# Experts of a mixture layer run before the last two rows of attention instead of behind all eight, and their results are gathered by token

## The chip, the core and the metric

The kernel runs on one core of a Trainium2 chip. The core has TensorE (PE, matrix products into PSUM), VectorE (DVE), ScalarE (ACT), GpSimd (POOL) and SyncE (SP, which here only issues transfers); they run their own instruction streams and meet through semaphores. The metric is the device time of one execution in microseconds (us), lower is better. The times below are medians of several executions; the trace comes from one profiled execution.

## What is computed

With x of 8 batch rows ("rows" below) of 512 tokens and 256 features, a layer norm feeds two branches that are both added to x: causal attention with 16 heads and a linear position bias, and a mixture of 8 experts.

```python
xn = _layernorm(x, axis=-1)
x = x + attn(xn, W_kqv, b_kqv, W_proj, b_proj, slopes) + ffn(xn, Wg, W1, W2)

# ffn, T = 4096 tokens, E = 8 experts, cap = T // E = 512
probs = softmax(xt @ Wg)
# every expert selects its cap likeliest tokens; a token goes to the likeliest expert
# that selected it, or to its likeliest expert if none did
out = sum over e of  where(tok2exp == e, weight, 0) * (gelu(xt @ W1[e]) @ W2[e])
```

Each token goes through exactly one expert, so the kernel sorts tokens by expert and computes 39 tiles of 128 sorted tokens (4096 tokens, up to 7 tiles of padding).

## The kernel before

**Start.** Layer norm of all rows, projections to keys, queries, values and the router's logits, each value split into a high and a low fp16 part. It ends 120.5 us into the trace, where the first exponential of attention starts.

**Eight rows of attention.** Each row has 4 groups of 4 heads, each group 10 slots (`NSJ`), so 40 slots a row. In a slot PE computes scores (`scores`, L1368), ACT takes their exponential into `pr_all` (L865), and in rows 0 to 5 POOL zeroes the part above the diagonal (L711, 7 selects a group); in rows 6 and 7 PE adds the mask to the scores itself (L1363). Slots of a later group hold the product with the values (`with_v`, L1388), transposes, the projection (L1418) and the residual add on DVE (L1052). In the same slots PE and DVE find the row maxima of the *next* row (`max_unit`, L1287 and L1293; `row_max`, L992 and L997), so row 7 has none of that work. Which slot holds what is a table; each engine's stream is in the order of the slots, and an engine that waits in one slot holds back all that is behind it in its stream.

**Work for the experts within the rows.** 32 quarters of expert weights are read, scaled by ACT (L834), split by POOL (`expert_high` L678, `expert_low` L682) and stored: 4 before row 0, then one a group in rows 0 to 6. DVE finds each expert's 512th chance by 15 bisection steps (`bisect_count`, `bisect_take`: 6 in row 0, 3 each in rows 1, 2 and 3), and then makes the routing, 18 pieces of small operations in rows 4 and 5 (`ROUTED = 4`). The list of sorted tokens is filled with empty entries by 10 DMAs of POOL in the start; then 32 scatters of POOL (indirect DMAs, 128 tokens each, L695) write normalized tokens with their number and weight into `sorted_rows`: four in a run behind each of the groups in `SCATTERS`, from (row 5, group 2) to (7, 1).

**Experts, behind row 7.** Per tile: SP loads a transposed tile (L488) and its 128 token numbers (L491), PE computes `up` (16 products, L1540 and L1541) and `down` (12 products, L1550), both with weight addresses from registers, and between them ACT and DVE pass five operations: `cross` (L889), `sum_up` (L1214), `gelu` (L895), `high` (L901), `low` (L1219). POOL gathers the 128 rows of x plus attention that belong to the tile (L744), DVE multiplies the result by the weight and adds them (`combine`, L1225), and POOL scatters the tile to the output (L750). `up` runs three tiles ahead of `down`. Hidden values use two pairs of PSUM banks; attention's buffers in `pr_all` hold the experts' inputs and results.

Of the kernel before, what the change touches and what calls it, by code (L numbers as in the profile page):

```python
# [22 lines left out]
AHEAD = 4  # L23
OUT_BANKS = (4, 6, 5, 7)
# [5 lines left out]
ROWS_FIRST = 3  # L30
ROWS_EARLY = 4
# [3 lines left out]
HG = 4  # L35
# [26 lines left out]
ROW = 2 * E + 4  # L62
BITS = 30
ROUTED = 4
SCATTERS = [(5, 2), (5, 3), (6, 0), (6, 1), (6, 2), (6, 3), (7, 0), (7, 1)]
PER_EXPERT = NT // X
FILLS = 10
FILLS_FIRST = 5

HALVES = 3  # L70
NO_TOKEN = 1 << 20
# [19 lines left out]
STEPS = [(0, u) for u in (1, 8, 15, 22, 29, 36)] + [(n, u) for n in range(1, ROUTED) for u in (2, 8, 14)]  # L91
# [15 lines left out]
GROUPS = NG * B  # L107
AWAY = GROUPS - 5


def values_at():
    pieces, copies, turns, scales, pairs, packs = ({} for _ in range(6))
    for y in range(GROUPS - 1):
# [6 lines left out]
        pieces[own_ + first], pieces[own_ + second] = (y, (0,)), (y, (1, 2, 3))  # L120
        copies[own_ + copy], turns[own_ + turn], scales[own_ + turn] = y, y, y
# [6 lines left out]
NQ = 4  # L128


def layer(nc, x, w_kqv, b_kqv, w_proj, b_proj, slopes, wg, w1, w2, out):
# [6 lines left out]
    out_rows = out.rearrange("b s e -> (b s) e")  # L138
    xa_t = xa_d.rearrange("(b t p) e -> b p t e", p=P, t=TB)

    with ExitStack() as ctx:
# [29 lines left out]
        x_last = tables[:, 0:TB * E].rearrange("p (t e) -> p t e", t=TB)  # L171
# [63 lines left out]
        def cut(n_bytes, dt, pattern=None, **dims):  # L235
# [15 lines left out]
        token = sb("token", [P, 8, 2], I32)  # L251
# [51 lines left out]
        pos_made, scattered, list_init, w1_in, w2_in = sem("pos_made"), sems("scattered", X), sem("list_init"), sem("w1_in"), sem("w2_in")  # L303
        xs_in, xT_in, h_made, hg_made, hh_made, hl_made, o_made, ob_made = (
            sems("xs_in", SLOTS), sems("xT_in", SLOTS), sem("h_made"), sem("hg_made"), sem("hh_made"),
            sem("hl_made"), sem("o_made"), sem("ob_made"))
        cross_out, h_summed = sem("cross_out"), sem("h_summed")
        xg_in, ob_out = sems("xg_in", SLOTS), sems("ob_out", SLOTS)
        consts = sem("consts")
        apart = sem("apart")  # L310
        zrows_in, bias_made, xb_made = sem("zrows_in"), sem("bias_made"), sem("xb_made")
        xr_made = sem("xr_made")
        x_last_in = sem("x_last_in")
# [8 lines left out]

        def wait_apart(eng, signal, value):
            eng.wait_ge(signal, value)
            eng.sem_inc(apart, 1)
# [25 lines left out]


# [11 lines left out]
        def _(sp):  # L364
# [96 lines left out]
            for n in range(B):  # L461
                for g in range(NG):
                    q = NQ * (n + 1) + g
                    if NQ < q <= NQ * X:
                        store_quarter(q - 1)
                    if NQ * X > q + 1 and q > NQ:
                        load_quarter(q + 1)
                    if g == 3 and n < B - 1:
                        shift_rows(n + 1)
# [25 lines left out]
            for q in range(ROWS_EARLY):  # L495
                load_rows(q, q)
                if q == 1:
                    store_sum(B - 2)
# [1111 lines left out]
```

## Time and profile before

| what | us |
|---|---|
| median of 3 executions (595.95 to 599.14) | 597.97 |
| span of the profiled execution, first to last instruction | 607.7 |
| start, to the first exponential of row 0 | 120.5 |
| rows 0 to 5 | 243.4 |
| rows 6 and 7 | 81.8 |
| last exponential of row 7 to the end | 162.0 |

The profiled execution's time is known by its span alone, which is 9.7 us over the median of the timed ones. Busy time in the span: PE 504.2, DVE 404.6, ACT 337.4, POOL 326.0. Boundaries of rows are the starts of their first exponential. In the trace, a number in square brackets is how long the engine had been idle before an instruction, and the arrow names what ended that; "remote" means that no instruction of the program ends at that moment, "issue" that the engine waited for nothing that the profile shows.

### The profile page before, as it was taken

Reading aid. Unit: us, or ns where it says so; the run is one execution under the profiler, and the core shown is the slowest. Engines: PE = TensorE matmul, PEld = TensorE weight load, DVE = VectorE, ACT = ScalarE, POOL = GpSimd, SP = SyncE. Lnnn points to the kernel's source line nnn. Section 1 sums busy time; section 2 is a strip of 40 time slices with the busy share of each in tenths; the row PEclk is TensorE's granted clock in tenths of the full one; section 3 lists DMA queues with packets and bytes.
Section 4 is the critical chain, followed back from the end, with each engine's and each line's share of the span. In section 5 each row is a group of like instructions: output and inputs, shape, how many; then the busy total and the mean of one; then the engine's idle time right before and its main releaser. Section 6 shows DMA issues by size and latency. Waiting matters only on the chain.

```text
span 607.7 us, 13176 instructions
## 1 busy us (share of the span) xinstructions
PE 504.2 (83%) x4807; PEld 288.6 (47%) x4807; DVE 404.6 (67%) x829; ACT 337.4 (56%) x640; POOL 326.0 (54%) x524
## 2 busy tenths in 40 slices
PE   1989996688889889899888898977897887887785
PEld 1555652233334444343434344433465676575664
DVE  5987769997998897987898976620124444354344
ACT  4455652165766676766757666555644444354343
POOL 4787634245535463644745568654413665555555
PEclk9999997558989999998999898998898898798889
DMA  8899998232413433525225238438355343333410
GB/s 264 266 243 269 303 310 267 91 92 62 126 62 115 148 118 100 149 79 146 84 84 148 81 105 254 151 101 310 114 106 124 100 107 83 94 94 100 94 56 35
DMA packets 94903, 85.59 MB, mean 141 GB/s; under 512 B 36883, under 2 KB 84883, under 8 KB 94831
## 3 DMA queue, kind: packets, MB, share of 16 engines
q1 hardware_dynamic: 82088, 59.64, 34.0%
q0 software_dynamic: 7360, 18.80, 10.4%
q10 hardware_dynamic: 5392, 6.31, 3.4%
q8 instruction: 39, 0.64, 0.4%
q14 instruction: 24, 0.20, 0.1%
HBM read 42.26 MB, written 37.95 MB: 132 GB/s over the span
## 4 chain that ended last, share of the span: by engine, by line
PE 50%; DVE 29%; issue 7%; ACT 6%; another core or an unknown queue 5%; POOL 3%; DMA 1%; ACTq 0%; DVEq 0%; POOLq 0%
DVE mx L997 12%; PE ps L1388 9%; PE ps L1256 8%; PE ps L1368 6%; PE ps L1550 6%; PE ps L1418 5%; PE ps L1540 4%; DVE mx L992 3%; PE ps L1541 3%; ACT pr_all L865 3%; PE ps L1293 3%; PE ps L1287 2%; PE ps L1398 2%; PE ps L1363 2%
## 5 line engine op out<-in xcount | busy, mean ns | idle before, releaser
L865 ACT ACTIVATE pr_all<-ps 128x512 f32<-128x512 f32 x320 | 179.1, 598 | 86.3 <-PE ps L1368 80.9
L997 DVE TENSOR_REDUCE mx<-ps 128x2 f32<-128x768 f32 (+1 forms) x192 | 156.9, 863 | 18.4 <-PE ps L1293 9.2
L711 POOL TENSOR_SCALAR_AFFINE_SELECT pr_all<-pr_all 128x256 f32<-128x256 f32 (+1 forms) x168 | 71.1, 451 | 115.2 <-ACT pr_all L865 115.1
L1368 PE MATMUL ps<-qs,ks 64*128 64x384 f16 (+3 forms) x512 | 108.6, 316 | 11.8 <-ACT pr_all L865 11.1
L1388 PE MATMUL ps<-pr_all,vt 128*17 128x512 f32 (+3 forms) x1024 | 88.3, 463 | 1.9 <-ACT pr_all L865 1.3
L1550 PE MATMUL ps<-vt,pr_all 128*128 x312 | 65.2, 295 | 20.3 <-DVE pr_all L1219 15.2
L1214 DVE TENSOR_TENSOR pr_all<-ps,pr_all 128x512 f32<-128x512 f32 x39 | 27.0, 691 | 75.2 <-ACT pr_all L889 52.9
L1293 PE MATMUL ps<-ks,qs 64*128 64x128 f16 (+3 forms) x512 | 76.8, 330 | 0.0
L1287 PE MATMUL ps<-step,pick 64*128 64x128 bf16 (+1 forms) x640 | 55.1, 223 | 22.9 <-DVE mx L997 15.6
L750 POOL DMA_INDIRECT out_dram<-pr_all,token x39 | 43.8, 1124 | 48.0 <-DVE pr_all L1225 32.7
L1540 PE MATMUL ps<-pr_all,xnp 128*128 128x256 f16 x312 | 61.6, 288 | 3.7 <-DVE pr_all L1214 2.7
L1541 PE MATMUL ps<-pr_all,xnp 128*128 128x128 f16 x312 | 58.4, 229 | 4.6 <-issue 4.6
L889 ACT ACTIVATE pr_all<-ps 128x512 f32<-128x512 f32 x39 | 23.1, 593 | 68.0 <-PE ps L1541 34.7
L1368 PEld LDWEIGHTS ps<-qs,ks 64*128 64x128 f16 x512 | 36.5, 98 | 51.0 <-ACT pr_all L865 38.0
L1287 PEld LDWEIGHTS ps<-step,pick 64*128 64x128 bf16 x640 | 27.5, 98 | 66.9 <-DVE mx L997 31.3
L744 POOL DMA_INDIRECT pr_all<-x_plus_attention,token x39 | 40.7, 1045 | 22.7 <-issue 11.6
L992 DVE TENSOR_REDUCE mx<-ps 128x4 f32<-128x1024 f32 x32 | 39.1, 1223 | 14.3 <-PE ps L1293 13.6
L1550 PEld LDWEIGHTS ps<-vt,pr_all 128*128 128x128 f16 x312 | 32.5, 105 | 29.3 <-DVE pr_all L1219 18.2
L1550 PE MATMUL ps<-w_low,pr_all 128*128 x156 | 45.8, 294 | 0.7 <-issue 0.7
L1388 PEld LDWEIGHTS ps<-pr_all,vt 128*17 128x17 f32 x1024 | 24.6, 99 | 37.4 <-issue 27.2
L1256 PE MATMUL ps<-pr_all,w_h 128*128 128x512 f16 x128 | 39.5, 391 | 1.3 <-ACT pr_all L783 1.3
L1540 PEld LDWEIGHTS ps<-pr_all,xnp 128*128 x312 | 32.3, 103 | 11.8 <-issue 6.5
(195 smaller groups left out, 885.2 us busy)
## 6 DMA issues: line engine op xcount, KB each, us to landing
qs<-q_parts SPq DMA_DIRECT2D x64, 100.0 KB
ks<-k_parts SPq DMA_DIRECT2D x64, 96.0 KB
sorted_rows<-ecmp POOLq DMA_DIRECT2D x10, 516.0 KB, 7.0
k_parts<-pr_all SPq DMA_DIRECT2D x16, 256.0 KB, 2.9
q_parts<-pr_all SPq DMA_DIRECT2D x16, 256.0 KB, 3.1
w_h<-in_L_ffn_W_dram SPq DMA_DIRECT2D x16, 256.0 KB
w_l<-in_L_ffn_W_dram SPq DMA_DIRECT2D x16, 256.0 KB
expert_parts<-w_low SPq DMA_DIRECT2D x32, 128.0 KB
```

The costliest lines, as they stand in the source:

```text
L711: pool.affine_select(out=v, in_=v, compare_op=ALU.is_ge, fill=0.0, base=0, pattern=[[0, blocks], [1, P]], channel_multiplier=-1).then_inc( ...
L865: act.activation(dst, src, ACT.Exp, scale=SCORE).then_inc(exp_made, 1)
L992: last = dve.tensor_reduce(mx[:, n1 % 2, :, 2 * g:2 * g + 2, 1], ps[:, 2 * (u % 2):2 * (u % 2) + 2, :].rearrange("p e (c n) -> p e c n", c=2),
L997: last = dve.tensor_reduce(mx[:, n1 % 2, :, 2 * g + c, t], ps[:, 2 * (u % 2):2 * (u % 2) + 2, c0:c0 + w], AX, ALU.max)
L1256: last = pe.matmul(out, lhs(a_, k), rhs(b_, k), start=(k == 0 and j == 0), stop=(k == EC - 1 and j == 2))
L1287: pe.matmul(dst[:, :, c0:c0 + HALF], pick64[own_half(e), h, :], step64[own_half(e), None, :].broadcast_to([HALF, len(ends), HALF]), start= ...
L1293: last = pe.matmul(bank[2 * (u % 2) + e][:, c0:c0 + w], qs[own_half(e), p1, 2 * g + i, P * t:P * (t + 1)], ks[own_half(e), p1, 2 * g + i, ...
L1368: last = pe.matmul(dst[:, c0:c0 + w], ks[rows, p, 2 * g + i, t * P:(t + 1) * P], qs[rows, p, 2 * g + i, t * P:S], start=not masked, stop=T ...
L1388: last = pe.matmul(bank[6][32 * h:32 * h + VW, t * P:S], vt[:, n, t, g * HG + h, :], pr_all[:, HG * (g % 2) + h, W_AT[t]:W_AT[t] + S - t * ...
L1540: pe.matmul(both, hi, xT[:, q8, k::EC, :], start=(k == 0), stop=(k == EC - 1), skip_group_check=True)
L1541: last = pe.matmul(own_, lo, xT[:, q8, k, :], start=False, stop=(k == EC - 1), skip_group_check=True)
L1550: last = pe.matmul(out[:, 0:E], hh[:, q, a_, f * P:(f + 1) * P], weights(w2_b[b_], e * W2_STEP + w2_at(f), E), start=(f == 0 and j == 0), ...
```

## The change

- The expert stage is moved between row 5 and row 6 (`SPLIT = 6`). It needs its routing sooner: the steps of the bisection are 6, 5, 4 in rows 0, 1, 2; all routing is in row 3 (`ROUTED = 3`); up to 6 quarters of weights a row in rows 0 to 3 and 4 in row 4.
- The 10 fills of the list follow the first 10 groups. The 32 scatters stand singly between the selects, four a group, in the groups (3, 3) to (5, 2). Token numbers and weights are no longer stored with the rows (`ROW` is 512 and not 516).
- In the expert stage POOL has no instruction. DVE copies each tile's result (`take_result`), and SP stores it to `sorted_results`, in sorted order.
- POOL waits until all 39 tiles are stored (`tiles_out`), then gathers 32 times 128 results by token, one every second slot of rows 6 and 7 (`GATHERS_AT`); six slots after its gather DVE multiplies by the weight and adds to x plus attention (`add_moe`, `MOE_AT`), reloaded to `sums` for rows 0 to 4. SP stores whole rows of the output.
- Before row 6 PE waits for the last results, ACT for `o_made`, and from the second group of row 6 ACT waits for `tiles_out`, since `pr_all` is shared.

```diff
+SPLIT = 6
-SCATTERS = [(5, 2), (5, 3), (6, 0), (6, 1), (6, 2), (6, 3), (7, 0), (7, 1)]
+SCATTERS = [(3, 3), (4, 0), (4, 1), (4, 2), (4, 3), (5, 0), (5, 1), (5, 2)]
+SCATTER_AFTER = (2, 5, 8, 10)
-STEPS = [(0, u) for u in (1, 8, 15, 22, 29, 36)] + [(n, u) for n in range(1, ROUTED) for u in (2, 8, 14)]
+STEPS = [(0, u) for u in (1, 8, 15, 22, 29, 36)] + [(1, u) for u in (2, 8, 14, 20, 27)] + [(2, u) for u in (2, 8, 14, 20)]
+GATHERS_AT = {at_slot(SPLIT, 2 * t): t for t in range(NT)}
+MOE_AT = {at_slot(SPLIT, 2 * t + 6): t for t in range(NT)}
...
# POOL, per group of rows 0 to 5
+                    def scatter_at(place):
+                        if (n, g) in SCATTERS:
...
+                            pool.wait_ge(exp_made, NSJ * G + SCATTER_AFTER[place])
+                            scatter(PER_EXPERT * SCATTERS.index((n, g)) + place)
...
# POOL, rows 6 and 7
+            def gather(t):
...
+                pool.indirect_dma_start(out=moe[t // (NT // 2)][:, t % (NT // 2), :], out_offset=None, in_=ys_d,
+                                        in_offset=bass.IndirectOffsetOnAxis(ap=pos[:, t:t + 1].bitcast(U32), axis=0)
+                                        ).then_inc(moe_in[t % SLOTS], 16)
+            add_bias(SPLIT - 1)
+            pool.wait_ge(tiles_out, 1)
...
# ACT
+                    if G == G_SPLIT:
+                        act.wait_ge(o_made, WORK)
+                    if G == G_SPLIT + 1:
+                        act.wait_ge(tiles_out, 1)
...
# DVE
+            def take_result(s):
...
+                dve.tensor_copy(ob[:, q, :], bank[OUT_BANKS[s % len(OUT_BANKS)]][:, 0:E]).then_inc(ob_made, 1)
...
# PE
+                if v in (NSJ * G_SPLIT, NSJ * G_SPLIT + 1):
+                    pe.wait_ge(ob_made, WORK - 2 + v % 2)
...
+            def experts():
+                turn_y(G_SPLIT - 2)
...
+                up(0, e[0])
+                with_v(G_SPLIT - 1, range(TB))
...
+                up(1, e[1])
+                turn_y(G_SPLIT - 1)
...
+                up(2, e[2])
+                turn_pair(G_SPLIT // 2 - 1)
```

Where work moves, in the order of the instructions. First POOL in row 4, one group with its selects (AFFINE_SELECT), its weight quarter (CAST, then TENSOR_TENSOR); `pos` is the list of places. Before:

```order
L711 AFFINE_SELECT pr_all<-pr_all 128x2x128 x3
L678 CAST vt<-w_h 128x512
L711 AFFINE_SELECT pr_all<-pr_all 128x2x128 x3
L711 AFFINE_SELECT pr_all<-pr_all 128x4x128
L682 TENSOR_TENSOR w_low<-w_h,vt 128x512
```

POOL in row 4, group 2, now:

```order
L716 DMA sorted_rows<-xnp,pos 5120x256
L730 AFFINE_SELECT pr_all<-pr_all 128x2x128 x3
L716 DMA sorted_rows<-xnp,pos 5120x256
L699 CAST vt<-w_h 128x512
L730 AFFINE_SELECT pr_all<-pr_all 128x2x128 x3
L716 DMA sorted_rows<-xnp,pos 5120x256
L730 AFFINE_SELECT pr_all<-pr_all 128x4x128
L716 DMA sorted_rows<-xnp,pos 5120x256
```

The same selects now have a scatter ahead of or behind each of them. Second, DVE at the routing's pieces `pick` to `choose` (operations on `rr`, `r` and `hit`), between the row maxima (`mx`). Before, in row 4:

```order
L1091 TENSOR_TENSOR rr<-rr,gtb 128x256
L997 TENSOR_REDUCE mx<-ps 128x2 x4
L1121 TENSOR_REDUCE r<-rr 128x32
L1091 TENSOR_TENSOR rr<-rr,r 128x256
L992 TENSOR_REDUCE mx<-ps 128x2x2
L997 TENSOR_REDUCE mx<-ps 128x2
L1042 RECIPROCAL rec<-ps 128x16
L1046 TENSOR_TENSOR yqp<-ps,rec 128x4x64
L1091 TENSOR_TENSOR rr<-rr,pr 128x256
```

The same pieces now, in row 3:

```order
L1110 TENSOR_TENSOR rr<-rr,gtb 128x256
L1140 TENSOR_REDUCE r<-rr 128x32
L1110 TENSOR_TENSOR rr<-rr,r 128x256
L1013 TENSOR_REDUCE mx<-ps 128x2
L1110 TENSOR_TENSOR rr<-rr,pr 128x256
L1145 SCALAR_TENSOR_TENSOR rr<-rr 128x256
L1149 TENSOR_REDUCE r<-rr 128x32
L1110 TENSOR_TENSOR rr<-rr,r 128x256
```

One row maximum stands where there were six. Third, PE where the expert stage now hands over to row 6, the last products of `down` and the first scores, masks and row maxima:

```order
L1542 MATMUL ps<-w_low,pr_all 128x256
L1542 MATMUL ps<-vt,pr_all 128x256
L1404 MATMUL ps<-id,late 128x64 x2
L1409 MATMUL ps<-qs,ks 128x512
L1326 MATMUL ps<-step,pick 128x64 x4
L1332 MATMUL ps<-ks,qs 128x512 x2
```

No product with the values stands in the first group of row 6, since that of row 5's last group is done within the expert stage.

## Rows read from the trace of the kernel before

**Rows 1.** Windows by stage: length, busy us by engine (instructions), granted clock, DMA share, GB/s.
```profile
core 0: us, PE busy (x) PEld busy (x) DVE busy (x) ACT busy (x) POOL busy (x), PEclk, DMA share, GB/s
...
161.70:203.40 41.70, 36.79 (x387) 17.22 (x387) 36.45 (x82) 27.09 (x51) 18.30 (x36) 0.96 0.33 102
203.40:242.70 39.30, 35.20 (x380) 16.61 (x380) 34.25 (x76) 27.20 (x52) 20.99 (x40) 1.00 0.41 124
242.70:281.90 39.20, 35.47 (x381) 16.66 (x381) 34.15 (x76) 27.09 (x52) 21.00 (x40) 1.00 0.38 113
281.90:324.10 42.20, 36.47 (x382) 16.70 (x380) 37.00 (x63) 27.09 (x51) 22.56 (x40) 0.96 0.35 102
324.10:363.90 39.80, 35.66 (x381) 16.98 (x381) 35.62 (x64) 27.22 (x52) 25.63 (x44) 0.96 0.37 110
363.90:408.50 44.60, 38.14 (x415) 19.27 (x415) 23.10 (x36) 27.07 (x51) 29.64 (x33) 0.96 0.53 175
408.50:445.70 37.20, 31.30 (x313) 14.39 (x313) 5.02 (x14) 24.02 (x47) 14.88 (x18) 0.91 0.57 190
...
460.60:602.60 142.00, 115.42 (x1046) 95.35 (x1044) 64.08 (x114) 65.04 (x113) 81.86 (x76) 0.91 0.35 88
```
**Rows 2.** Timeline of PE: first product of down for two tiles in a row.
```profile
543.67 0.27 PE L1550 MATMUL ps<-vt,pr_all 128*128 x1
...
546.30 0.27 PE L1550 MATMUL ps<-vt,pr_all 128*128 x1
```
**Rows 3.** Timeline of POOL, ACT and PE at one stop of the expert stage.
```profile
559.77 1.03 POOL L744 DMA_INDIRECT pr_all<-x_plus_attention,token  x1 [0.30 <-issue]
...
565.09 1.03 POOL L744 DMA_INDIRECT pr_all<-x_plus_attention,token  x1 [0.30 <-issue]
...
567.18 0.60 ACT L889 ACTIVATE pr_all<-ps 128x512 f32<-128x512 f32 x1 [4.87 <-remote]
...
562.69 0.22 PE L1541 MATMUL ps<-pr_all,xnp 128*128 128x128 f16 x1
```
**Rows 4.** Timeline of POOL and DVE in row 6: last of four scatters, next row maximum.
```profile
369.83 0.97 POOL L695 DMA_INDIRECT sorted_rows<-xnp,pos  x1 [0.30 <-issue]
...
371.80 1.29 DVE L997 TENSOR_REDUCE mx<-ps 128x2 f32<-128x768 f32 x2 [3.33 <-remote]
```
**Rows 5.** The chain that ended last, shares by line: expert stage, then rows 6 and 7.
```profile
by line: PE ps L1550 24.8%; another core or an unknown queue 17.3%; PE ps L1540 15.2%; issue 12.7%; PE ps L1541 11.4%; DVE pr_all L1214 5.9%; DVE pr_all L1219 5.3%; ACT pr_all L889 4.3%; ACT pr_all L901 1.7%; DVE pr_all L1225 1.1%; POOL out
...
by line: PE ps L1368 17.3%; PE ps L1388 15.3%; PE ps L1363 12.4%; ACT pr_all L865 10.1%; issue 9.9%; PE ps L1418 7.1%; another core or an unknown queue 6.9%; PE ps L1398 6.2%; PE ps L1293 5.3%; ACT ysb L839 3.8%; PE ps L1287 2.8%; PE ps L14
...
by line: PE ps L1388 19.2%; PE ps L1368 16.3%; issue 15.8%; ACT pr_all L865 14.5%; PE ps L1363 11.4%; PE ps L1418 10.4%; PE ps L1398 7.2%; another core or an unknown queue 4.9%; ACT ysb L839 2.3%; PE ps L1405 1.6%; ACT yqp L845 1.2%
```
**Rows 6.** Groups of DVE instructions in row 2: three bisection steps.
```profile
L1074 DVE TENSOR_SCALAR_CACHE_REDUCE hit<-rr,cand 128x256 bf16<-128x256 f32 x3 | 1.4, 479 | 0.1
...
L1084 DVE TENSOR_TENSOR thr<-thr,found 128x1 uint32<-128x1 uint32 x3 | 1.0, 335 | 0.1
...
L1070 DVE TENSOR_TENSOR cand<-thr,bits 128x3 uint32<-128x3 uint32 x3 | 0.6, 215 | 0.1
```
**Rows 7.** Groups of POOL instructions: row 4, and the scatters of rows 6 and 7.
```profile
L711 POOL TENSOR_SCALAR_AFFINE_SELECT pr_all<-pr_all 128x256 f32<-128x256 f32 (+1 forms) x28 | 12.8, 484 | 19.7 <-ACT pr_all L865 19.6
L691 POOL TENSOR_TENSOR xr<-xr,xb 128x256 f32<-128x256 f32 x4 | 2.8, 729 | 0.0
...
L682 POOL TENSOR_TENSOR w_low<-w_h,vt 128x512 f16<-128x512 f32 x2 | 2.3, 1156 | 0.0
...
L678 POOL CAST vt<-w_h 128x512 f16<-128x512 f32 x2 | 1.2, 606 | 0.0
...
L695 POOL DMA_INDIRECT sorted_rows<-xnp,pos x28 | 27.4, 978 | 10.2 <-issue 7.0 <-ACT pr_all L865 3.1
```
**Rows 8.** The end of row 7 in the chain and on DVE, and 256 KB stores' landing.
```profile
446.35 2.35 PE ps L1388 x32
448.70 1.92 PE ps L1418 x8
...
455.20 1.53 DVE L1236 TENSOR_TENSOR tables<-ps,tables 128x512 f32<-128x512 f32 x2 [1.91 <-PE ps L1418]
...
q_parts<-pr_all SPq DMA_DIRECT2D x16, 256.0 KB, 3.1
```

More of the change, by code:

```diff
@@ L698, in _ @@
             pool.wait_ge(bias_made, 1)
-            for part in range(FILLS_FIRST, FILLS):
-                empty_list(part)
             for q in range(NQ):
@@ L703, in _ @@
                 expert_low(q)
-            for n in range(B):
+            for n in range(SPLIT):
                 for g in range(NG):
@@ L773, in _ @@
+            add_bias(SPLIT - 1)
+            pool.wait_ge(tiles_out, 1)
+            for n in range(SPLIT, B):
+                for g in range(NG):
+                    for k in range(NSJ):
+                        if (n, g, k) in GATHERS_AT:
+                            pool.wait_ge(exp_made, NSJ * (NG * n + g) + k)
+                            gather(GATHERS_AT[n, g, k])
+                    if n == SPLIT and g > 1:
+                        add_bias(SPLIT + g - 2)
         @block.scalar
@@ L915, in _ @@
+            copy_y(NG * B - 1)
+            copy_pair(GROUPS // 2 - 1, slice(0, S // 2))
         @block.vector
@@ new lines, in experts, with add_moe @@
+            def experts():
+                scale(G_SPLIT - 2)
+                for s in range(HID):
+                    sum_up(s)
+                    low(s)
+                    if s == 0:
+                        scale(G_SPLIT - 1)
+                for s in range(WORK):
+                    if s + HID < WORK:
+                        sum_up(s + HID)
+                    if HID <= s + HID - 1 < WORK:
+                        low(s + HID - 1)
+                    take_result(s)
+            def add_moe(t):
+                n = t // TB
+                dve.wait_ge(moe_in[t % SLOTS], 16 * (t // SLOTS + 1))
+                if n < SPLIT - 1:
+                    dve.wait_ge(sums_in[n], 16)
+                elif n == SPLIT - 1:
+                    dve.wait_ge(xadd_made, t + 1)
+                else:
+                    dve.wait_ge(xr_made, n + 1)
+                rows = sum_rows(n)[:, t % TB, :]
+                dve.scalar_tensor_tensor(out=rows, in0=moe[t // (NT // 2)][:, t % (NT // 2), :], scalar=r32[:, 3, t:t + 1],
+                                         in1=rows, op0=ALU.mult, op1=ALU.add).then_inc(moe_added, 1)
@@ L1560, in _ @@
             pe.wait_ge(xadd_made, TB * (B - 1))
-            e = [expert(code[s // SLOTS], s % SLOTS) for s in range(WORK)]
-            find_up(0)
             with_v(NG * B - 1, range(TB))
```

549 lines of the change are left out of this document (271 added, 278 removed).

## The prediction, made before the changed kernel ran

> **What bounds the kernel now.** I read the busy time by stage first [rows 1]. In rows 2 and 3 of attention PE is busy 35.2 to 35.5 us and DVE 34.2 of some 39.2, and the length of a row follows DVE: 34.2 busy gives 39.2, 37.0 gives 42.2. Row 7, without row maxima, leaves DVE at 5.0 of 37.2. The expert stage, from the first `down` at 460.6 to the last at 602.6, takes 142.0 us for 39 tiles, 3.64 a tile. Two neighbouring tiles in the timeline start 2.63 apart, with PE full [rows 2]; 39 of those are 102.6. So 39 us of this stage are stops.
>
> The stops have one look [rows 3]. The last product of an `up` is recorded to end at 562.9, and ACT, which needs nothing more, starts only at 567.18, "remote", after 4.87 idle. POOL had issued five indirect DMAs without a pause, the last from 565.09 to 566.12: the stop ends 1.1 us after it. Row 6 has the same: four scatters, the last ending at 370.80, and a row maximum that begins at 371.80 after 3.33 idle [rows 4]. I found this end, 1.0 to 1.2 us behind a run of indirect DMAs, at every long stop I looked at in rows 6, 7 and the experts. In the chain these places are "unknown queue" and "issue", 17.3% and 12.7% of the expert stage, 6.9% and 4.9% "unknown queue" in rows 6 and 7 [rows 5]. My reading: PE's signals are held while POOL's indirect DMAs run in a row. What holds them I can't see.
>
> **The experts without POOL.** Between row 5's last exponential and row 6's first, PE has one `with_v` (2.35, [rows 8]), three sets of four transposes (some 0.6 each, an estimate from the fp32 products beside them), and 39 tiles by 2.63: 2.4 + 1.8 + 102.6 = 106.8. To that comes the first load of transposed rows, which SP issues only after `with_v` of group 22 (about 1.5), and at the end, where no `up` is left to cover them, the five operations from `up` to `down` (about 2), a copy and the first score (1): **112**. ACT and DVE have some 1.9 us a tile and stay below 2.63. SP's 128 KB store a tile is cheap to issue and nothing waits for it but `tiles_out`. The bounds are 108 (all ends overlap) and 151 (the 39 us stay).
>
> **The end.** From the last exponential at 445.7 to the last residual add at 456.7 [rows 8] are 11.0, of which `up` of two tiles took 3.0 of PE; they leave. Then a 256 KB store: 0.4 to issue and 3.1 to land [rows 8]. Tail: 11.0 − 3.0 + 3.5 = **11.5**. Before, the tail was inside the 162.0 behind row 7.
>
> **Rows 1 to 5, DVE.** One step of the bisection is three marks of 0.48, 0.34, 0.21 and two small ones: 2.3 us [rows 6]. Row 1 gets two more, +4.7; row 2 one more, +2.3. Row 3 loses three steps (−7.0), which leaves a bare 27.2; the routing, read as what rows 4 and 5 have over the bare load, is 9.8 + 8.4 = 18.2 [rows 1]. DVE in row 3 is then 45.4, 11.3 over now, and the row about 50.5. Rows 4 and 5 lose the routing, but they can't fall below PE's 35.5 and its gaps: I take 38.5 each, −3.7 and −1.3. Moving DVE's work costs because it's heaped: sum **+13.3**. If the heap in row 3 partly fills DVE's idle 5 us, it is +7.
>
> **Row 4, POOL.** Selects 12.8, bias 2.8, four quarters of 1.76, and 16 of the scatters at 0.98 plus the 0.30 of idle between them: 12.8 + 2.8 + 7.0 + 20.5 = 43.1 us [rows 7] in a row of 38.5. Each select stands behind a scatter, and `with_v` waits for the selects; POOL becomes the bound there: **+5**. Row 3 (4 scatters) and row 5 (12, no quarters: 31) stay under. The signals held by 32 single scatters: no row shows single ones. The bounds are 0 and the expert stage's 39 us over 78 indirect DMAs, 0.5 each, 16; I take **+2**, since in row 5 now four cost nothing visible against row 3 [rows 1]. ACT's and POOL's fills and quarters are covered: ACT is idle 12 us a row.
>
> **Rows 6 and 7** were 81.8. Out go one `with_v` (2.4, counted above) and the held signals behind runs of scatters, 6.9% of 44.6 and 4.9% of 37.2, 4.9 together. In come: (a) the restart. POOL's first gather waits for `tiles_out`, about 4 us after the last result, and lands some 3 later; DVE's first `add_moe` is six slots into row 6, about 5 us, and behind it stand row maxima that PE needs: +3. (b) 32 gathers of 1.03, one every second slot, that is, every 2 us: denser than single scatters, thinner than the runs. Bounds 0 and 0.5 each, 16: I take +5. (c) 32 adds of 0.48 on DVE, 15 us, hidden in its 21.5 and 32 idle us. Together 81.8 − 7.3 + 8 = **82.5**.
>
> **The sum,** against the trace's span: up to row 1 161.7; rows 1 to 5 202.2 + 13.3 + 5 + 2 = 222.5; experts 112; rows 6 and 7 82.5; tail 11.5. That is 590.2, 17.5 under 607.7. The timed executions have a median 9.7 below the span; I carry the difference over whole: 598.0 − 17.5 = 580.5, rounded to **581**. The start is left as it is: its last 23 us are DVE's row maxima, and the five fills taken from it are DMA work beside PE's.
>
> **Rivals.** *The stops stay* (ends slower). PE's stops would be a matter of its own stream in the expert stage, with addresses from registers, and not of POOL. Then the stage takes 151 rather than 112 and the time is 620, and the change has only costs: +20 in rows 1 to 5, +8 in rows 6 and 7. It turns slower than before once more than some 17 of the 39 us stay. For it: I see signals held, not by what. Against: row 6 has no register addresses and shows the same stop with the same end [rows 4].
> The Trainium skill speaks for this rival: the page "SBUF — State Buffer", section "SBUF: two separate sides", says that of the engines only DVE and GpSimd contend, and that "PE, ACT, and DVE's dedicated pair never wait on anyone". By that rule POOL's DMAs could not hold PE, and the result would be this rival's 620; the rows speak against it, as far as they show a cause.
>
> *The gathers hold what the scatters held.* If 32 gathers cost the expert stage's 0.5 each or, being dense, nearly 1, rows 6 and 7 take 93 to 110, and the time is 592 to 608. For it: POOL is again in indirect DMAs for more than half of two rows. Against: they stand two slots apart, and in row 6 the first two scatters of the run delayed nothing.
>
> *The heap in rows 3 and 4 is dearer.* Each routing piece now holds PE's row maxima; PE may wait for DVE and then DVE for PE. If row 3 takes 56 and row 4 48, the time is 590.
>
> *The heap and the gathers are nearly free.* DVE's extra +7, POOL's 0, held signals 0, restart 0: 581 − 6 − 5 − 2 − 8 = 560.
>
> **Chances.** Forecast (572 to 588) 0.42; cheap case (558 to 572) 0.20; dear rows (588 to 595) 0.14; gathers that hold, beyond 595, 0.10, half of it within 0.5%; stops that stay 0.14, nearly all slower. The range is from 562 to 604: it leaves out the lower end of the cheap case and the rival of 620, 2 in 10 together. A difference of 0.5%, 3 us, is about what a measurement of this kernel can tell from none. Faster by more: 0.42 + 0.20 + 0.14 + 0.04 = 0.80; within it 0.06; slower 0.14.
>
> **What would show it.** In the profile of the changed kernel: `down` of tiles starting 2.6 to 2.7 us apart throughout and the "remote" waits of ACT's first operation gone; the expert stage near 112 from exponential to exponential. Row 3 near 50 with DVE full; row 4 near 44 with POOL full and PE waiting for selects. One wait of DVE at its first `add_moe`. If rows 6 and 7 show "remote" waits a microsecond behind gathers, the second rival holds; if tiles still take 3.6 us with POOL idle, the first does, and my reading of the stops is wrong.

## The result, and the profile after

The changed kernel takes 648.97 us (median of 4, 647.26 to 653.41) beside 598.56 for the kernel before (595.95 to 603.15): the ratio is 1.084, with an interval from 1.077 to 1.090. It is 50 us slower, where 17 us less were forecast. The profiled execution, the longest of the four, has a span of 651.7 (first to last instruction).

The windows by stage of the changed kernel, as [rows 1] has them of before (length, then busy us by engine with instructions, granted clock, DMA share, GB/s): rows 0 to 5, the expert stage, rows 6 and 7, the end.

```profile
121.00:172.10 51.10, 32.53 (x331) 14.07 (x331) 39.32 (x98) 27.36 (x51) 27.32 (x48) 0.80 0.43 138
172.10:230.50 58.40, 42.61 (x385) 19.32 (x383) 39.02 (x101) 28.57 (x52) 24.48 (x44) 0.82 0.38 122
230.50:284.70 54.20, 40.46 (x380) 18.26 (x375) 37.05 (x86) 28.47 (x53) 25.80 (x46) 0.85 0.38 115
284.70:353.10 68.40, 45.18 (x390) 19.55 (x389) 45.32 (x82) 28.55 (x53) 29.83 (x48) 0.77 0.27 82
353.10:401.30 48.20, 38.95 (x380) 17.75 (x376) 28.50 (x42) 27.21 (x51) 34.36 (x53) 0.87 0.49 157
401.30:444.30 43.00, 37.86 (x374) 17.73 (x374) 28.88 (x43) 25.83 (x48) 28.15 (x46) 0.88 0.63 209
444.30:553.60 109.30, 107.03 (x1145) 95.49 (x1144) 65.33 (x122) 72.18 (x124) 3.86 (x5) 1.00 0.44 106
553.60:602.40 48.80, 36.81 (x370) 18.01 (x368) 29.80 (x49) 24.49 (x44) 24.74 (x27) 0.83 0.55 179
602.40:639.00 36.60, 31.28 (x313) 14.92 (x313) 11.25 (x28) 23.95 (x47) 12.80 (x14) 0.91 0.25 78
639.00:651.60 12.60, 7.36 (x56) 4.75 (x56) 2.60 (x6) 1.03 (x3) 0.00 (x0) 1.00 0.20 70
```

| stretch | before | forecast | after |
|---|---|---|---|
| to the start of row 1 | 161.7 | 161.7 | 172.1 |
| rows 1 to 5 | 202.2 | 222.5 | 272.2 |
| expert stage | within "end" | 112 | 109.3 |
| rows 6 and 7 | 81.8 | 82.5 | 85.4 |
| end | 162.0 | 11.5 | 12.6 |
| span | 607.7 | 590.2 | 651.7 |

The expert stage did what was forecast. PE is busy 107.0 of its 109.3 us, and the products of `down` run from 453.3 to 552.8, 99.5 us, where before they took 142.0 [rows 1]:

```profile
L1542 PE MATMUL ps<-vt,pr_all x312: 269/273/283, 453.3 to 552.8; 128*128 x156
```

The miss is 61.5 us of span, and 60 of them lie before the stage. (In the medians it is 68: the prediction took the median to lie 9.7 us below the span, and it lies 2.7 below.) In rows 1 and 2 PE is idle for 15.8 and 13.7 us a row and DVE for 19.4 and 17.2, while before it was some 4 to 5 each [rows 1]. So no engine is full there; something starves all of them.

**What starves them.** The SP queue's own waits over rows 0 to 4 (queue, line, what it waited for: us in total, times, longest), then those of PE and ACT there:

```profile
SPq L452 <- POOL w_low L703: 108.5, 18, 17.3
...
PE ps L1409 <- DMA qs<-cc: 24.4, 3, 8.7
...
ACT w_l L847 <- DMA w_l<-in_L_ffn_W_dram: 23.1, 6, 6.6
...
ACT w_h L847 <- DMA w_h<-in_L_ffn_W_dram: 9.8, 4, 6.2
```

L452 is SP's `store_quarter`, L1409 the scores, L847 the scaling of a quarter. With two quarters in groups 1 and 3, SP's stream holds: store the last quarter, load the next, store the *first quarter of this group*, load again, and only then `shift_rows` (L371, `qs<-cc`), which brings the next row's maxima to PE. POOL splits the first quarter of a group only behind the group's last select. So SP stands in the second store for the whole group, and the shift stands behind it. The timelines of SP, ACT and POOL at the end of row 2:

```profile
268.97 0.43 SPq L444 DMA_DIRECT2D w_l<-in_L_ffn_W_dram  x1
279.23 0.33 SPq L452 DMA_DIRECT2D expert_parts<-w_low  x1
279.60 0.43 SPq L444 DMA_DIRECT2D w_h<-in_L_ffn_W_dram  x1
280.08 2.41 SPq L371 DMA_DIRECT2D qs<-cc  x4
...
276.79 0.60 ACT L917 ACTIVATE pr_all<-ps 128x512 f32<-128x512 f32 x1
...
284.68 0.60 ACT L917 ACTIVATE pr_all<-ps 128x512 f32<-128x512 f32 x1 [7.30 <-PE ps L1409]
...
278.05 1.15 POOL L703 TENSOR_TENSOR w_low<-w_h,vt 128x512 f16<-128x512 f32 x1
```

Row 2's last exponential starts at 276.79. POOL's split ends at 279.20, SP's store goes out at 279.23, the shift at 280.08, and row 3 starts at 284.68. Rows 1 to 4 all begin so: the last groups of rows 0 to 3, with the stop behind them, take 17.9 to 22.4 us. The load behind such a second store is the other half of it: ACT is to scale that quarter behind the second exponential of the next group. At this place the late shift covers the load (279.60), and ACT does not wait for it. Behind group 1 of each row nothing covers it: there ACT waits 4.4 to 6.6 us for that load, 26 of the 33 us in 10 waits that it has for quarters in rows 0 to 4.

**What the stops cost on top.** The same place in windows of 2 us; the seventh number is the clock granted to TensorE:

```profile
274.00:276.00 2.00, 2.00 (x28) 0.72 (x26) 0.83 (x3) 0.60 (x1) 1.12 (x3) 1.00 0.00 0
...
278.00:280.00 2.00, 0.00 (x0) 0.00 (x0) 0.00 (x0) 0.00 (x0) 1.92 (x4) 1.00 0.00 0
280.00:282.00 2.00, 0.00 (x0) 0.00 (x0) 0.00 (x0) 0.00 (x0) 0.99 (x1) 0.58 0.65 202
...
284.00:286.00 2.00, 2.00 (x10) 0.50 (x10) 0.32 (x1) 0.60 (x1) 0.00 (x0) 0.50 0.59 207
...
290.00:292.00 2.00, 2.00 (x9) 0.15 (x8) 1.95 (x4) 0.60 (x1) 0.96 (x3) 0.50 0.95 237
```

PE stops at 277, its clock falls from 2.4 to 1.2 GHz between 280 and 282, and it is still at 1.2 at 292, some 7 us after the work has come back. Taking twice (1 − clock) times the length of each window as time at the lower level, rows 0 to 5 have 31 us of it before and 112 us now, and PE's busy time in them rises from 214.4 to 237.6 for the same work.
The Trainium skill's page "TensorE: Matmul & The Clock Gate", section "HAM oscillation — how this bites in real kernels", describes this pattern with waits for DMAs, and prices it at half of the time at the lower clock. By that rule 81 us more would cost 40 us; the rows show PE busy for 23 more, so here it is the direction that agrees and not the size.

### The profile page after: what moved, and what is told of

Read it like the earlier page. It is cut to its first block, busy times and chain, and to the rows that moved or that the text cites. A ratio compares the mean times of both kernels' runs of the same rounds, so it can differ in the third digit from the quotient of the medians.

```text
span 651.7 us, 13061 instructions
## 1 busy us (share of the span) xinstructions
PE 514.8 (79%) x4807; PEld 292.7 (45%) x4807; DVE 420.4 (65%) x860; ACT 341.8 (52%) x642; POOL 270.6 (42%) x475
## 4 chain that ended last, share of the span: by engine, by line
PE 57%; DVE 12%; DMA 8%; issue 7%; POOL 7%; ACT 5%; SPq 3%; another core or an unknown queue 0%; DVEq 0%; POOLq 0%; ACTq 0%
PE ps L1429 11%; PE ps L1542 8%; PE ps L1295 7%; PE ps L1409 7%; PE ps L1532 5%; DVE mx L1013 5%; PE ps L1459 5%; PE ps L1332 4%; ACT pr_all L917 3%; DMA w_l<-in_L_ffn_W_dram 3%; PE ps L1533 3%; POOL pr_all L730 2%; PE ps L1326 2%; PE ps L1439 2%; POOL w_low L703 2%
## 5 line engine op out<-in xcount | busy, mean ns | idle before, releaser
L1409 PE MATMUL ps<-qs,ks 64*128 64x512 f16 (+3 forms) x512 | 119.8, 336 | 69.2 <-ACT pr_all L917 32.4
L1429 PE MATMUL ps<-pr_all,vt 128*17 128x512 f32 (+3 forms) x1024 | 94.1, 490 | 1.1 <-ACT pr_all L917 0.9
L1409 PEld LDWEIGHTS ps<-qs,ks 64*128 64x128 f16 x512 | 38.1, 100 | 118.2 <-issue 58.7
L1332 PE MATMUL ps<-ks,qs 64*128 64x128 f16 (+3 forms) x512 | 85.8, 353 | 0.0
L1326 PE MATMUL ps<-step,pick 64*128 64x128 bf16 (+1 forms) x640 | 60.4, 232 | 25.5 <-DVE mx L1013 11.6
L770 POOL DMA_INDIRECT w_low<-sorted_results,pos x16 | 15.4, 964 | 108.5 <-SPq L533 95.0
L1542 PE MATMUL ps<-vt,pr_all 128*128 x312 | 57.5, 273 | 0.9 <-DVE pr_all L1215 0.7
L1532 PE MATMUL ps<-pr_all,xnp 128*128 128x256 f16 x312 | 55.7, 273 | 1.4 <-DMA pr_all<-sorted_rows 1.4
L1459 PE MATMUL ps<-wp,yqp 128*128 128x256 f32 x128 | 40.6, 448 | 2.8 <-issue 1.1
L1542 PE MATMUL ps<-w_low,pr_all 128*128 x156 | 42.5, 273 | 0.0
L716 POOL DMA_INDIRECT sorted_rows<-xnp,pos x32 | 31.9, 996 | 11.6 <-ACT pr_all L917 7.1
L852 ACT ACTIVATE ysb<-ps 128x512 f32<-128x512 f32 x32 | 19.1, 597 | 32.7 <-PE ps L1429 30.1
```

Source lines behind the costliest of these rows:

```text
L1326: pe.matmul(dst[:, :, c0:c0 + HALF], pick64[own_half(e), h, :], step64[own_half(e), None, :].broadcast_to([HALF, len(ends), HALF]), start= ...
L1332: last = pe.matmul(bank[2 * (u % 2) + e][:, c0:c0 + w], qs[own_half(e), p1, 2 * g + i, P * t:P * (t + 1)], ks[own_half(e), p1, 2 * g + i, ...
L1409: last = pe.matmul(dst[:, c0:c0 + w], ks[rows, p, 2 * g + i, t * P:(t + 1) * P], qs[rows, p, 2 * g + i, t * P:S], start=not masked, stop=T ...
L1429: last = pe.matmul(bank[6][32 * h:32 * h + VW, t * P:S], vt[:, n, t, g * HG + h, :], pr_all[:, HG * (g % 2) + h, W_AT[t]:W_AT[t] + S - t * ...
L1459: last = pe.matmul(dst, yp[:, (2 * n + i) % HALVES, t * P:(t + 1) * P], wp[:, i, :], start=(begin and i == 0), stop=(i == 1), skip_group_c ...
L1532: pe.matmul(both, hi, xT[:, q8, k::EC, :], start=(k == 0), stop=(k == EC - 1), skip_group_check=True)
```

## The experiments

Times are medians; ratios are to the kernel before, run beside it on the same chip. That kernel's own medians were 598.5 to 608.0 us from one set of runs to the next, so where two kernels of different sets are compared, a difference of a few us is left to the ratios. The diffs show the lines that matter and not the whole edit. Run 1 to run 4 are the kernels of sections 1 to 4.

**1. The order in SP's queue.** The shift goes ahead of the second quarter.

```diff
                     for late in range(2):
+                        if g == 3 and late:
+                            shift_rows(n + 1)
                         if (n, g, late) in QUARTERS_AT:
...
-                    if g == 3:
-                        shift_rows(n + 1)
```

> The changed kernel with one edit in SP's stream: in the last group of each row the loads of the next row's shifts (qs<-cc) are issued ahead of the second weight quarter's store and load, not behind them. Theory (SP's order): the changed kernel's rows 0 to 4 grew because SP waits there for POOL's split of a quarter (66 us of waits in 2.4 rows' time), and the shifts that row n+1's first scores need stand behind that wait; the last groups of rows 0 to 3, 18 to 22 us now, should lose 6 to 9 us each, the time fall from 649 to about 620. Rival (DVE's and POOL's heaped work is what stretches the rows): no group changes by over 1 us and the time stays at 649.

Measured: 632.49 us, ratio 1.053 (1.045 to 1.060). The shift was a cause, 16.5 us of it (some 18 by the ratios), and not the 29 that were hoped for. The last groups of rows 0 to 3, with the stop behind them, fell from 17.9, 22.4, 17.9 and 20.4 us (the start of one row's last group to the start of the next row) to 9.4, 15.2, 10.5 and 11.8. But the rows that now start earlier meet the load of the quarter: ACT's waits for it in rows 0 to 4 rose from 33 us to 50, and the first groups of rows 1 to 3 from 10.0, 9.7 and 12.3 to 14.3, 15.2 and 15.4. One late transfer had hidden the other.

**2. The load that ACT meets.** On top of run 1 ACT scales a group's first quarter behind the fifth exponential.

```diff
-                        for late, place in enumerate((1, 6)):
+                        for late, place in enumerate((4, 6)):
```

> As e1_shift_first, and ACT scales the first quarter of a group behind the fifth exponential and not the second, so that it no longer waits in the second slot for a load that SP could issue only at the end of the group before. Theory (SP's order): the groups behind a group with two quarters, 17 us now in rows 1 to 4, fall to 11 to 13, and the time by another 15 to 25 us against e1_shift_first, to about 600. Rival (those groups are long because ACT and POOL have more quarters): they stay at 17 and the time equals e1_shift_first's.

Measured: 609.18 us, ratio 1.011 (1.003 to 1.018). One number in a table is worth 23 us; ACT's waits for quarters are 31 us, spread over 16. The first groups of rows 1 to 3 fall to 12.2, 10.7 and 10.2 us; the third groups of rows 1 to 4, which were to fall to 11 to 13, stand at 16.0, 15.0, 12.9 and 12.7. The two edits together take 39.8 of the 50 us back (the ratio goes from 1.084 to 1.011).

**3. The heap of quarters.** From the changed kernel, without runs 1 and 2: the 28 quarters spread over rows 0 to 5, and with them the last store two groups later and one load of weights one group later.

```diff
-QUARTERS = [(n, g, late) for n in range(4) for g in range(NG) for late in range(1 + g % 2)] \
-    + [(4, 1, 0), (4, 1, 1), (4, 2, 0), (4, 3, 0)]
+QUARTERS = [(n, g, late) for n in range(SPLIT) for g in range(NG) for late in range(2)
+            if (not late or (g == 1 and n < 5) or (n, g) == (0, 2)) and (n, g) < (5, 2)]
```

> The changed kernel with its 28 quarters of weights spread over rows 0 to 5, one a group and a second one only in the second group of rows 0 to 4 and the third of row 0, instead of two in every second group. SP's and ACT's order within a group is the changed kernel's. Theory (SP's order): the last groups of rows 1 to 3 fall to some 11 to 12 us, since no second quarter stands ahead of the shifts there; the groups behind a second group stay at 17; time about 615. Rival (number of quarters in rows 0 to 3): rows 0 to 3 shrink by 1.2 us for each quarter taken out, under 15 us in all.

Measured: 624.72 us, ratio 1.036 (1.027 to 1.045). With one quarter in group 3, SP has no second store ahead of the shift, and the last groups of rows 0 to 3 fall to 14.0, 15.1, 10.5 and 11.8 us: the late shift is undone here by another way than in run 1. The time is 10 us over the 615 expected: the third groups stay long (14.7 to 20.8 us in rows 0 to 4), and the stage has grown from 109.3 to 112.9.

**4. Both ways at once.** The even quarters, ACT scaling behind the fifth exponential, and the shift ahead of all the quarters of the last group.

> The three edits of the earlier runs together: 28 quarters of weights about one a group over rows 0 to 5, SP issues the next row's shift ahead of a group's quarter, and ACT scales a quarter behind the fifth exponential of its group and not behind the second. Theory (PE is starved by SP's queue order and by loads that ACT meets too early; PE's clock falls after each stop and makes it longer): what the heap of quarters costs and what the late shift costs are different waits, so the gains add in part. Rows 1 to 3 took 152.5 us with shift and scale moved, of which row 1 had 52.6; with even quarters they should take 142 to 147, row 4 44 rather than 46.4, and the time 598 to 603, granted clock in rows 1 to 5 at 0.92 or more. Rival (what is left in rows 1 to 3 is DVE's heap, bisection and routing, alone): even quarters add nothing, 607 to 611.

Measured: 609.49 us, ratio 1.016 (1.010 to 1.022), beside 609.18 and 1.011 without the even quarters. The rival holds on the time: the gains don't add. Rows 1 and 2 are 6 us shorter than in run 2, but row 0 is 3.4 longer and the expert stage 3.4 longer. Of the stage's 3.4, 2 are at its start: PE waits 3.6 us for what its first `up` needs, where it waited 1.7 in run 2. Whether that is its last weights or its first rows, and why row 0 is longer, the runs don't show.

**5. Do indirect DMAs hold PE's signals?** Three kernels put idle transfers of POOL into the expert stage of the changed kernel, where it has none, and one puts plain transfers in the place of the indirect ones in the stage of the kernel before. That one moves the same bytes but rows in order, so it leaves out the routing by token. The idle gathers, two a tile:

```diff
+            for s in range(WORK):
+                pool.wait_ge(h_made, s + 1)
+                for i in range(2):
+                    q = (2 * s + i) % SLOTS
+                    after(pool, idle_in[q], (2 * s + i) // SLOTS * 16)
+                    pool.indirect_dma_start(out=spare[:, q, :], out_offset=None, in_=xs_d.bitcast(F32),
+                                            in_offset=bass.IndirectOffsetOnAxis(ap=pos[:, s % NT:s % NT + 1].bitcast(U32), axis=0)).then_inc(idle_in[q], 16)
```

> The changed kernel with two indirect gathers per tile added on POOL in the expert stage (128 rows of 1 KB each from sorted_rows to a part of SBUF that nobody reads), as many as the kernel before had there. Nothing on PE, ACT or DVE waits for them. Theory (signals of PE are held by runs of indirect DMAs): the stage, 110 us from the last exponential of row 5 to the first of row 6, grows by 20 to 50 us, and ACT's first operation of a tile shows remote waits of 2 to 5 us. Rival (the stops of the kernel before came from its DVE and SP waits on gathers and scatters, which nobody waits for here): the stage stays at 108 to 114 us.

> The changed kernel with 78 idle transfers of POOL in the expert stage, two a tile, as in the run with idle gathers, but plain ones of 128 rows by 1 KB, not indirect; nobody waits for them but tiles_out. The idle gathers made the stage about 37 us longer, with 43 us of remote waits at ACT's first operation. If it is the indirect form that holds PE's signals: stage 110 to 114 us, time near 650. If any transfer that POOL issues does it, or the added bytes: stage 140 or more, time near 680.

> The changed kernel with 39 idle indirect gathers in the expert stage, one a tile and not two. If every gather costs the same, half of 37 us: stage about 128, time near 668. If only gathers close behind each other hold the signals (in rows 6 and 7 of the changed kernel, one every 2 us, nothing of it is seen): stage 110 to 115, time near 650 to 655.

> The kernel before, with the 78 indirect DMAs of its expert stage (gather of x plus attention and scatter of the output) replaced by plain ones of the same bytes, rows in order and not by token number; so each token's sum is taken and stored for the wrong token. Reading of the prediction (39 of the stage's 142 us are signals held by indirect DMAs): tiles start 2.63 apart throughout, the stage from first to last down takes 103 to 106 us, the remote waits of ACT's first operation (26.9 us) go, time 560 to 566. Rival (the stops belong to any DMA of POOL, or to PE's own stream): 590 or more.

Measured: 682.14, 649.87 and 661.16 us for the first three (one execution each), and 561.41 for the kernel before with plain transfers, beside 602.10 unchanged. The products of `down` in those four, in this order (count, duration, first to last start); behind the first and the last a fence with ACT's wait at the operation `cross` in the stage:

```profile
L1554 PE MATMUL ps<-vt,pr_all x312: 269/273/417, 447.2 to 584.0; 128*128 x156
```
```profile
ACT pr_all L876 <- remote: 43.4, 19, 19.1
```
```profile
L1553 PE MATMUL ps<-vt,pr_all x312: 269/273/283, 448.7 to 548.2; 128*128 x156
```
```profile
L1554 PE MATMUL ps<-vt,pr_all x312: 269/273/418, 452.5 to 559.8; 128*128 x156
```
```profile
L1548 PE MATMUL ps<-vt,pr_all x312: 272/273/283, 455.7 to 555.7; 128*128 x156
```
```profile
ACT pr_all L887 <- PE ps L1539: 21.5, 33, 1.0
```

| kernel | POOL's transfers in the stage | first to last `down`, us | over 99.5, mean of each |
|---|---|---|---|
| changed | none | 99.5 | |
| changed | 78 plain, two a tile | 99.5 | 0 |
| changed | 39 indirect, one a tile | 107.3 | 0.20 |
| changed | 78 indirect, two a tile | 136.8 | 0.48 |
| before | 78 indirect | 142.0 | 0.54 |
| before | 78 plain | 100.0 | |

So the stops come with the indirect transfers and not with transfers of POOL as such, nor with their bytes or packets (78 of either form are 3744 packets and 10.23 MB), nor with PE's own stream: nobody waited for the idle gathers but `tiles_out`, and they stretched the stage by 37 us, with 43.4 us of remote waits that the changed kernel does not have. In the kernel before, 78 plain transfers in their place bring the stage to 100.0, take the remote waits (26.9 us there) away, and the time falls by 40.7 us (561.41 is one execution). The plain ones also read and write rows in order, so the indirect form and the scattered addresses are not told apart.

The means of the last column hide what matters: only gathers without a pause between them cost. POOL comes late to the stage, since it adds a bias first, and works its backlog off in one run. First the kernel with one gather a tile, its run of eight and a window of what follows (columns as in the windows above), then the one with two a tile, its run of sixteen:

```profile
461.97 1.37 POOL L785 DMA_INDIRECT pr_all<-sorted_rows,pos  x1 [0.15 <-issue]
...
471.50 0.95 POOL L785 DMA_INDIRECT pr_all<-sorted_rows,pos  x1 [0.30 <-issue]
...
473.83 0.60 ACT L876 ACTIVATE pr_all<-ps 128x512 f32<-128x512 f32 x1 [3.90 <-remote]
...
481.40:556.40 75.00, 75.00 (x795) 68.26 (x793) 46.08 (x85) 49.82 (x86) 27.45 (x29) 1.00 0.56 137
```
```profile
459.01 1.00 POOL L785 DMA_INDIRECT pr_all<-sorted_rows,pos  x1 [0.15 <-issue]
...
477.90 0.95 POOL L785 DMA_INDIRECT pr_all<-sorted_rows,pos  x1 [0.30 <-issue]
...
482.17 0.60 ACT L876 ACTIVATE pr_all<-ps 128x512 f32<-128x512 f32 x1 [19.12 <-remote]
```

With one a tile the whole 7.8 us lie at the run of eight: in the 75 us behind it, with 29 single gathers, PE is busy all the time. With two a tile one stop of 19.1 us, behind the run of sixteen, is half of the 37; the rest comes beside pairs and fours, where ACT's remote waits are at most 2.1 us each. By what path POOL's indirect DMAs hold another engine's signals no view shows.
The Trainium skill's rule that the prediction set against its own reading ("SBUF — State Buffer", section "SBUF: two separate sides": PE never waits on anyone) would, taken as broadly as the prediction took it, have all six rows of this table alike. They aren't; but that rule is on the ports of SBUF, and what the runs show is when PE's work is seen by others, so they decide against this use of it and say nothing of the ports.

**6. The restart in row 6.** In the changed kernel DVE stops 7.8 us at its first `add_moe`, six slots into row 6, and PE and ACT behind it. On top of run 4 the additions come later, and then the gathers too.

```diff
-MOE_AT = {at_slot(SPLIT, 2 * t + 6): t for t in range(NT)}
+MOE_AT = {at_slot(SPLIT, 2 * t + 16): t for t in range(NT)}
```

> The kernel of the run before, and the additions of the experts' results (add_moe) stand 16 slots behind their gather rather than 6, with SP's shift for row 7 ahead of the store of row 2. Theory: the stop of 8 us in the second group of row 6 (DVE waits in slot 6 for a gather that lands 5.4 us after tiles_out, PE for DVE's row maximum, ACT for PE) is a wait of DVE at its first addition alone: the group goes from some 18 us to 11, and the time falls by 6 to 7 us. Rival: the stop is moved, since the gathers come as late for the additions that follow, or ACT's wait for tiles_out takes its place: less than 2 us.

Measured: 612.47 us, ratio 1.022 (1.016 to 1.027), no gain. The second group of row 6 fell from 18.1 to 14.7 us, the third rose from 11.7 to 14.5. The rival was right on the time, in a form that it had not named. DVE's longest wait in row 6, and POOL, with the last of nine gathers:

```profile
DVE mx L1013 <- remote: 6.3, 1, 6.3
```
```profile
535.83 0.94 POOL L770 DMA_INDIRECT w_low<-sorted_results,pos  x1 [0.30 <-issue]
```

When `tiles_out` came, ACT was ten slots into row 6, and POOL, at 1.25 us a gather, had its backlog worked off only with the ninth, 0.30 us between each and the next. DVE's stop ended at 537.85, 1.1 us after the last of them: the run of indirect DMAs had only taken the place of the late addition.

This run shows the clock too. In row 4, where the two programs are the same, the last group of run 4 and that of this run:

```profile
346.90:358.00 11.10, 10.19 (x107) 5.09 (x107) 7.52 (x13) 7.09 (x13) 8.57 (x13) 1.00 0.66 204
```
```profile
350.50:365.50 15.00, 14.44 (x107) 6.70 (x107) 7.81 (x14) 7.29 (x13) 8.43 (x13) 0.68 0.52 157
```

The same 107 products keep PE busy for 10.19 us at a full clock and 14.44 at a mean of 0.68, and the group is 3.9 us longer. Why the clock fell in one and not in the other I did not find; it makes up half of the 7.5 us by which row 5 starts later here.

For the next kernel, called run 6 below, gathers and additions are both moved, the quarters end a group sooner (with second ones in other groups), and ACT scales later. These are three edits at once, told apart only by where they act.

```diff
-GATHERS_AT = {at_slot(SPLIT, 2 * t): t for t in range(NT)}
-MOE_AT = {at_slot(SPLIT, 2 * t + 16): t for t in range(NT)}
+GATHERS_AT = {at_slot(SPLIT, 2 * t + 11): t for t in range(NT)}
+MOE_AT = {at_slot(SPLIT, 2 * t + 17): t for t in range(NT)}
...
-                        for late, place in enumerate((4, 6)):
+                        for late, place in enumerate((7, 9)):
```

> The kernel of the run with additions later, with three edits: gather t stands in slot 2t + 11 and its addition in slot 2t + 17, so that POOL has no backlog of gathers when tiles_out comes; the quarters end in (5, 0), one group sooner, with two in groups 1 and 3 of row 0; ACT scales behind the eighth and tenth exponential of a group, not the fifth and seventh. In the run before, DVE's first addition no longer stopped, but a run of nine gathers without a pause followed, and a remote stop of 6.3 us of DVE and 6.5 of ACT ended 1.1 us after the last of them. Theory (a run of indirect DMAs holds the signals, and TensorE's clock then falls to half for several us): with a gather every other slot the remote stop goes, the second and third group of row 6 take 11 and 12 us and not 14.7 and 14.5, row 6 takes 40 rather than 45, the stage 110 and not 115; time 596 to 603. Rival (the stop is not from the run of gathers, but from reloading sums or from tiles_out itself): row 6 stays at 45, time 605 or more.

Measured: 598.41 us (10 executions), ratio 0.995 (0.992 to 0.998). Row 6 takes 39.2 us rather than 45.3, its second and third groups 9.0 and 11.0, and the granted clock there is 1.00; the stage, the gap between the last exponential of row 5 and the first of row 6, is 111.8 and not 115.1; rows 0 to 4 give the other 8 us back. DVE has a remote wait of 3.1 us left, behind a run of four gathers.

**7. The heap on DVE.** On top of run 6, three bisection steps left out, so that the thresholds are coarser; then all 15 kept, but placed early in rows 0 to 2, and 7, 4 and 4 of them in these rows rather than 6, 5 and 4.

```diff
-STEPS = ... [(1, u) for u in (2, 8, 14, 20, 27)] + [(2, u) for u in (2, 8, 14, 20)]
+STEPS = ... [(1, u) for u in (2, 8, 14)] + [(2, u) for u in (2, 8, 14)]
```

> The kernel of the paced gathers without three of the 15 steps of the bisection, the last two of row 1 and the last of row 2, so that both rows have three steps as in the kernel before; the thresholds are then coarser and some tokens go to another expert. DVE's work left out is 7 us. Theory (the heap on DVE sets rows 1 and 2, and stops with a fallen clock make it dearer than its busy time): row 1 goes from some 50 us to 42 or 43, row 2 from 44 to 40, time 10 to 12 us under that of the paced gathers. Rival (rows 1 and 2 are long because of weight quarters and SP's order, and the steps fill idle time): less than 4 us.

```diff
-STEPS = [(0, u) for u in (1, 8, 15, 22, 29, 36)] + [(1, u) for u in (2, 8, 14, 20, 27)] + [(2, u) for u in (2, 8, 14, 20)]
+STEPS = [(0, u, r) for u, r in ((1, 5), (6, 10), (11, 15), (16, 20), (21, 25), (26, 32), (33, 37))] \
+    + [(n, u, u + 4) for n in (1, 2) for u in (1, 6, 11, 16)]
```

> The kernel of the paced gathers with the 15 bisection steps placed otherwise: 7, 4 and 4 in rows 0, 1 and 2 rather than 6, 5 and 4, one every 5 slots and not every 6 or 7, so that rows 1 and 2 have theirs in groups 0 and 1 and none in groups 2 and 3, where the residual adds stand. The run with three steps less brought row 1 from 49.6 to 38.9 us and row 2 from 43.8 to 39.2, that is 4.6 to 5.3 us a step whose DVE work is 2.3. Theory (a step costs its work where DVE has idle time left, and twice that in groups 2 and 3, where PE stops and its clock falls): row 1 at 41 to 43, row 2 at 41 to 42, row 0 at 47 to 48, time 589 to 594. Rival (a step costs 5 us anywhere, or the shorter interval makes PE wait for DVE's marks): rows 1 and 2 gain what groups 0 and 1 lose, time 596 to 600.

Measured: 585.60 us with three steps less (one execution), 12.8 under run 6; and 593.00 with the steps early, ratio 0.979 (0.971 to 0.986). Windows of rows 1 and 2 of run 6, of the kernel with three steps less, and of that with the steps early:

```profile
166.00:215.60 49.60, 41.58 (x377) 18.33 (x377) 37.77 (x101) 28.14 (x52) 22.91 (x42) 0.83 0.47 150
215.60:259.40 43.80, 36.94 (x382) 17.44 (x382) 36.43 (x87) 28.12 (x53) 24.89 (x45) 0.96 0.47 148
```
```profile
166.00:204.90 38.90, 35.34 (x375) 16.49 (x375) 33.74 (x79) 28.01 (x53) 22.88 (x42) 0.96 0.58 180
204.90:244.10 39.20, 35.38 (x381) 16.65 (x381) 34.26 (x76) 28.03 (x53) 24.91 (x45) 1.00 0.56 178
```
```profile
165.20:207.50 42.30, 36.09 (x381) 16.63 (x380) 36.12 (x87) 28.10 (x53) 24.13 (x44) 0.96 0.55 171
207.50:250.50 43.00, 36.56 (x382) 16.95 (x382) 36.76 (x87) 28.09 (x52) 24.80 (x45) 0.96 0.50 157
```

Two steps in groups 2 and 3 of row 1 cost 10.7 us for 4.0 us of DVE's time. DVE holds a row maximum there, PE stops, and its clock falls (0.83 against 0.96, PE's busy time 41.6 against 35.3). The chain that ended last passes through a step there, between two row maxima, in run 6:

```profile
183.88 1.13 DVE mx L1008
...
185.42 0.53 DVE thr L1103
...
187.43 0.40 DVE rr L1093 x2
187.83 1.15 DVE mx L1013
```

With four steps in the first half, row 1 takes 42.3. How much of that is the place and how much the step that went to row 0 is not told apart: row 2, with the same four steps moved early, gains only 0.8 (43.8 to 43.0), and row 0 takes its seventh step without growing (45.0 to 44.5). Against the kernel with three steps less, the fourth step costs row 1 3.4 us and row 2 3.8 even when placed early. This is the version that beats the kernel before most clearly: 2.1% under it, with all the work done.

## Why the prediction was wrong

- **What bounds the kernel: right.** The stops belong to POOL's indirect DMAs in a run, as read from where they end; the four kernels of section 5 show it in both directions. One count was off: from the first to the last `down` lie 38 intervals, not 39, so the stops before were 42 us and not 39.
- **Expert stage 112: right,** 109.3. **End 11.5: right,** 12.6. **Rival "the stops stay": wrong,** though its side of the outcome came true, by luck: the kernel is slower for another reason.
- **The step that failed** is one sentence: "ACT's and POOL's fills and quarters are covered: ACT is idle 12 us a row." It asks whether the engines have time, and never in what order SP's queue meets the quarters. The cover failed twice: the shift stood behind a store that waits for POOL, and ACT waited for a load sent late. Runs 1 and 2 show that these two places alone are 42.2 of the 61.5 us of the miss, with the fallen clock in it (span 651.7 to 609.5). Row 0, left as it was in the sum, grew by 10 us, and with both edits is back to 42.5.
- **DVE's heap, +18.3 in rows 1 to 3** (4.7 + 2.3 + 11.3): mis-sized. With SP's order mended, run 6 has 146.8 us there against 120.2 before, +26.6. Each term was taken as DVE's busy time, and that was forecast well (45.4 in row 3, measured 45.3); what was wrong is its price: row 1's two steps measured 10.7 and not 4.7. Row 3, at 53.4, lies between the forecast's 50.5 and the 56 of the rival with the dearer heap. That rival's mechanism is shown for the bisection steps; for the routing it is not tested: the second group of row 3, where pieces of it stand, takes 17.5 to 18.4 us in every version. Row 4, which the rival had at 48, takes 44.5.
- **Rows 4 and 5: 82 forecast, 83.5 in run 6.** The sizes were right. POOL is busy 40.2 of row 4's 44.5 us there, but the chain that ended last goes through two loads of a quarter in that row too, for 10.8 us, and no run takes the scatters out, so that POOL bounds it is not shown. The near-nothing of single scatters fits row 5, 39.0 us with 12 of them.
- **Rows 6 and 7: 82.5 forecast, 85.4 measured.** The restart is the term that was mis-sized: +3 in the sum, 7.8 us of DVE's wait in the trace. The gathers at one every other slot cost less than the 5 allowed, as run 6 shows, whose rows 6 and 7 take 77.0 with all 32 of them; only their backlog costs.
- **No term for the clock** stood in the sum. With stops this long it is no small matter: 81 us more at the lower level.

## What to carry to other kernels

When work is moved forward, follow each queue that it is moved past in the order of its own stream, SP's first: an engine that is idle 12 us a row can still be the one that everyone waits for, because one store waits for it ahead of a load that others need. Size a stop on PE's path by what PE's clock does afterwards, not only by its length. And where an engine waits "remote", look for indirect DMAs that run back to back. Plain ones in their place took 41 us off the kernel before, which is what such runs cost there and not a gain to be had, since it left the routing out. One gather every 2.6 us cost nothing in the expert stage; pacing was not tried in the kernel before.

## What the runs showed of the hardware

- 78 indirect DMAs of POOL, 128 rows of 1 KB each, two a tile of 2.6 us, stretched a stage in which nobody waits for them from 99.5 to 136.8 us; 39 of them to 107.3; 78 plain ones of the same size, with rows in order, not at all. What costs is the run without a pause: one of sixteen held ACT for 19.1 us, one of eight cost 7.8, and 29 single ones, 2.6 us apart, nothing (PE busy 75.0 of 75.0 us). After a run of nine, DVE's stop ended 1.1 us behind the last; after the run of sixteen, ACT's ended 3.3 behind.
- A stop of 7 us of PE (277 to 284) was followed by at least 7 us of work at 1.2 GHz. The same 107 products took 10.19 us of busy time at a granted clock of 1.00 and 14.44 at 0.68.
